# Batch 1's 4x4 normalisation carried out during batch 0's attention, its products and sums on GpSimd

## What is computed

```python
# layer 0
x = x + attention0(xn) + streams(xn)       # one head of width 128; streams: four of 128 channels
def streams(xn):
    z = (rms_norm(xn) @ W_res.T).reshape(B, T, 4, 4) + H_res_base
    H = sinkhorn(z)                        # 50 iterations: rows, then columns, to sum 1 (tau 0.1)
    H = (1 - g) * eye(4) + g * H           # g = sigmoid(gate)
    mixed = einsum('btij,btjc->btic', H, xn_streams)
    return mixed + einsum('btc,btn->btnc', y, H_post)    # y = (streams weighted by H_pre) @ W_branch
# layer 1
x = x + attention1(xn) + ffn1(xn)          # 32 heads, 8 key-value heads of 128, causal; gated low-rank ffn
```

## Time and profile before

| | us |
|---|---|
| median of three runs | 2467.94 |
| lowest, highest | 2463.57, 2469.21 |
| the profiled execution | 2463.85 |
| its span in the trace | 2461.6 |

### The profile page before, as it was taken

The page is one execution under the profiler, slowest core; times in us unless marked ns, Lnnn a source line. Parts: engine busy times, 40 slices in busy tenths (PEclk is TensorE's granted clock), DMA queues, the critical chain, the costliest instruction groups (busy, mean ns, idle before and its releaser), DMA issues. The chain is left out here.

```text
span 2461.6 us, 35450 instructions
## 1 busy us (share of the span) xinstructions
PE 2233.0 (91%) x11154; PEld 1814.2 (74%) x11154; DVE 1554.9 (63%) x3685; ACT 1046.4 (43%) x2182; POOL 1012.0 (41%) x1038
## 2 busy tenths in 40 slices
PE   5767449899999999999999796999999999999998
PEld 4633137688888888888887684788888888888886
DVE  4289875466666666666766455566565756566665
ACT  4322213354545444454545232444454545454543
POOL 2644351264545455363634100435262525343341
PEclk9878779899999999999999998999999999999999
DMA  9500035501010101101010434201101010101010
GB/s 341 189 9 1 0 140 209 207 26 66 9 65 9 65 26 48 56 17 56 26 48 1 166 131 185 86 27 43 47 21 51 26 56 13 60 9 60 18 38 31
DMA packets 74003, 164.83 MB, mean 67 GB/s; under 512 B 4704, under 2 KB 38880, under 8 KB 67296
## 3 DMA queue, kind: packets, MB, share of 16 engines
q1 hardware_dynamic: 73504, 162.69, 18.8%
q10 hardware_dynamic: 432, 1.32, 0.1%
HBM read 113.14 MB, written 72.61 MB: 75 GB/s over the span
## 5 line engine op out<-in xcount | busy, mean ns | idle before, releaser
L1521 DVE TENSOR_TENSOR pT<-psum,pT 128x512 fp32r<-128x512 f32 x576 | 387.0, 689 | 282.4 <-ACT pT L1562 281.6
L1474 POOL TENSOR_TENSOR probs_even<-probs_even,rinv 128x1024 f32<-128x1024 f32 (+2 forms) x192 | 241.0, 1255 | 677.5 <-DVE rinv L1512 677.5
L1562 ACT ACTIVATE pT<-psum 128x512 fp32r<-128x512 f32 x576 | 329.2, 596 | 299.1 <-PE psum L1615 299.0
L1507 DVE CUSTOM_DVE_ANT_0 psum<-psum,causal 128x256 f32<-128x256 f32 (+7 forms) x512 | 386.0, 767 | 38.1 <-PE psum L95 33.3
L1474 POOL TENSOR_TENSOR probs_odd<-probs_odd,rinv 128x896 f32<-128x896 f32 (+2 forms) x192 | 198.6, 1042 | 303.0 <-DVE rinv L1512 302.9
L1556 ACT ACTIVATE probs_even<-psum,nmax 128x1024 f32<-128x1024 f32 (+3 forms) x256 | 204.5, 799 | 250.1 <-DVE nmax L1507 246.2
L93 PE MATMUL psum<-keys,q 128*128 128x512 f32 (+3 forms) x768 | 265.6, 346 | 3.7 <-DVE q L1495 2.8
L95 PE MATMUL psum<-keys,q 128*128 128x512 f32 (+3 forms) x768 | 262.0, 341 | 0.0
L94 PE MATMUL psum<-keys,q 128*128 128x512 f32 (+3 forms) x768 | 261.9, 341 | 0.0
L93 PE MATMUL psum<-pT,vals 128*128 128x512 f32 x576 | 256.3, 445 | 3.9
L1556 ACT ACTIVATE probs_odd<-psum,nmax 128x896 f32<-128x896 f32 (+3 forms) x256 | 176.7, 691 | 148.1 <-DVE nmax L1507 145.9
(11 more groups left out here) (272 smaller groups left out, 4410.5 us busy)
## 6 DMA issues: line engine op xcount, KB each, us to landing
k_parts<-kv_out SPq DMA_DIRECT2D x32, 512.0 KB, 4.9
wq<-wq_copy SPq DMA_DIRECT2D x16, 1024.0 KB, 4.8
wo<-wo_copy SPq DMA_DIRECT2D x16, 1024.0 KB, 4.8
v_parts<-kv_out SPq DMA_DIRECT2D x32, 512.0 KB, 3.9
keys<-k_parts SPq DMA_DIRECT2D x32, 512.0 KB, 4.8
vals<-v_parts SPq DMA_DIRECT2D x64, 256.0 KB, 3.1
acc<-in_x SPq DMA_DIRECT2D x4, 1024.0 KB, 12.3
xn_later<-xn SPq DMA_DIRECT2D x1, 2048.0 KB, 14.5
```

Source lines behind the costliest of these rows:

```text
L1474: pool.tensor_tensor(p, p, rinv[:, u, h:h + 1].to_broadcast([P, (TB - u) * P]), ALU.mult).then_inc(p_ok, 1)
L1507: dve.tensor_tensor_reduce(out=row, in0=row, in1=causal[:, S - n:S], scale=-1.0, scalar=-2 * MASKED, op0=ALU.add, op1=ALU.min, accum_out=n ...
L1521: dve.tensor_tensor(pT[:, n % PT_SLOTS, 1, :], bank[T_BANK + n % 2], f32(pT[:, n % PT_SLOTS, 0, :]), ALU.subtract).then_inc(t_lo, 1)
L1562: act.activation(pT[:, n % PT_SLOTS, 0, :], bank[T_BANK + n % 2], ACT.Copy).then_inc(t_hi, 1)
```

## The change

Batch 1's half of the normalisation leaves the loop of `layer0_mix`. The loop's parts now have four tiles each, the exponentials of batch 1 are put into buffers of their own (z1, k1), and 27 halves lie between units. The heads of a unit are added 14 halves into the next; those of the last unit fall in the mixing behind the loop. That mixing covers six tiles on VectorE and two (BY_POOL) on GpSimd, which waits for the closed T.

In the attention of batch 0, iterations 0 to 4 carry 20, 20, 18, 20 and 20 half-iterations for batch 1's eight tiles. GpSimd takes one after each scaling it does from u = 1 on (u = 2 in iteration 2): product, sum of pairs, sum of the two. VectorE takes the reciprocal of 32 sums behind its next `norm` step. Before iteration 2 ScalarE takes Ln of both factors, VectorE recentres z1 and ScalarE takes Exp; in iteration 5 VectorE closes T for batch 1. The mixing of batch 1's tiles moves to iterations 5 (three tiles), 6 (three) and 7 (two), one product and one sum after a scaling, with u = 1 included; before, it was one tile an iteration, a product and a sum after head 2 from u = 2 on. Their loads move within `loads`. VectorE's and ScalarE's instructions of batch 0's attention are written out instead of looped.

```diff
@@ -27,6 +27,7 @@
 TAU = 0.1
 SINKHORN_ITERS = 50
 SINKHORN_CHUNK = 25
+LATER_CHUNKS, LATER_HALVES = (20, 29), (20, 20, 18, 20, 20)
...
         def part_of(x, k):
-            return x[:, k * (NT // PARTS):(k + 1) * (NT // PARTS)]
+            return x[:, k * (TB // PARTS):(k + 1) * (TB // PARTS)]
...
-        PER_UNIT = 23
+        PER_UNIT = 27
+        BY_POOL = 2
...
+            pool.wait_ge(mix_ok, 1)
+            for t in range(TB - BY_POOL, TB):
+                x = x1[:, t, :].rearrange("p (i c) -> p i c", i=NS)
+                pool.wait_ge(x1_ok, t + 1)
+                for j in range(NS + 1):
+                    n = 2 * ((NS + 1) * (t - (TB - BY_POOL)) + j)
+                    stream = xn[:, t, j * D:(j + 1) * D] if j < NS else y[:, t, :]
+                    weight = T[:, t, :, j] if j < NS else rw[:, t, 1, :]
+                    if j == NS:
+                        pool.wait_ge(y_ok, t // 4 + 1)
+                    if n:
+                        pool.wait_ge(pooled, n)
+                    pool.tensor_tensor(product[:], stream.unsqueeze(1).to_broadcast([P, NS, D]),
+                                       weight.unsqueeze(2).to_broadcast([P, NS, D]), ALU.mult).then_inc(pooled, 1)
+                    pool.wait_ge(pooled, n + 1)
+                    pool.tensor_tensor(x, x, product[:], ALU.add).then_inc(pooled, 1)
...
-            after(dve.tensor_tensor(Z[:], Z[:], over_cols(v), ALU.subtract))
+            after(dve.tensor_tensor(Z[:, 0:TB], Z[:, 0:TB], wide_cols(v[:, 0:TB]), ALU.subtract))
+            after(dve.tensor_tensor(m.z1[:], Z[:, TB:NT], wide_cols(v[:, TB:NT]), ALU.subtract))
...
@@ -516,16 +537,15 @@
                 unit, k = t // UQ, t % UQ
                 between.setdefault(PER_UNIT * unit + 4 * k, []).append((maximum, t))
                 between.setdefault(PER_UNIT * unit + 4 * k + 3, []).append((invert, t))
-                behind = PER_UNIT * (unit + 1) + 16 if unit + 1 < UNITS else 2 * sum(CHUNKS) - UQ
-                between.setdefault(behind + k, []).append((add_heads, t))
+                between.setdefault(PER_UNIT * (unit + 1) + 14 + k, []).append((add_heads, t))
...
-            mixes = 0
-            last_op = {t: (x1_ok, t + 1) for t in range(NT)}
-            for k in range(0, TB, 2):
+            mixes, at = 0, 2 * sum(CHUNKS)
+            ready = {t: (x1_ok, t + 1) for t in range(NT)}
+            for k in range(0, TB - BY_POOL, 2):
                 for j in range(NS + 1):
                     for t in (k, k + 1):
                         if j == NS:
                             dve.wait_ge(y_ok, t // 4 + 1)
-                        dve.wait_ge(*last_op[t])
+                        dve.wait_ge(*ready[t])
...
-                        last_op[t] = mixed, mixes
+                        ready[t] = mixed, mixes
+                        for step, unit_tile in between.pop(at, ()):
+                            step(unit_tile)
+                        at += 1
+            assert not between, (at, between)
...
-            act.activation(K[:], Z[:], ACT.Exp).then_inc(k_ok, 1)
+            act.activation(K[:], Z[:, 0:TB], ACT.Exp).then_inc(k_ok, 1)
+            act.wait_ge(chain, at + 8)
+            act.activation(m.k1[:], m.z1[:], ACT.Exp)
...
-                        if t == 8:
-                            logs()
                 if unit:
                     act.wait_ge(pv_mm, TB * unit)
                     act.activation(oT[:], bank[6][:], ACT.Copy).then_inc(o_ok, 1)
+                if unit == 1:
+                    logs()
...
+            tiles_of = {5: (0, 1, 2), 6: (3, 4, 5), 7: (6, 7)}
+
+            def halves_of(it):
+                return iter(range(sum(LATER_HALVES[:it]), sum(LATER_HALVES[:it + 1])))
+
+            def first_pause(it):
+
+                return 2 if it == turning else 1
+
+            def factors(half):
+
+                return half + 1 + (half >= 2 * LATER_CHUNKS[0])
...
-            def loads(it, g):
+            def loads(it, g, mixed_now=()):
 
                 sp.wait_ge(q_mm, it * QS + QS)
                 load(wq[:, 1], m.wq_s[g]).then_inc(wq_in, 16)
+                for t in mixed_now[:2]:
+                    later_loads(t + 1)
                 sp.wait_ge(pv_mm, it * TILES + (PV0 + first_tile(4)))
                 for k in range(2):
                     load(vals[:, k, 4:8, :], vals_of(g, k, 1)).then_inc(v_in[1], 16)
+                for t in mixed_now[2:]:
+                    later_loads(t + 1)
...
-                loads(it, it + 1)
-                if mixes_later:
-                    later_loads(it + 1)
+                loads(it, it + 1, tiles_of.get(it, ()) if mixes_later else ())
+            if mixes_later:
+                later_loads(TB - 1)
...
@@ -1454,7 +1504,6 @@
                         pool.wait_ge(mixed, n)
                     pool.tensor_tensor(product[:], stream.unsqueeze(1).to_broadcast([P, NS, D]),
                                        weight.unsqueeze(2).to_broadcast([P, NS, D]), ALU.mult).then_inc(mixed, 1)
-                    yield
                     pool.wait_ge(mixed, n + 1)
                     pool.tensor_tensor(x, x, product[:], ALU.add).then_inc(mixed, 1)
                     yield
@@ -1472,15 +1521,36 @@
                         p = probs[u % 2][:, h, 0:(TB - u) * P]
                         pool.wait_ge(p_inv, it * SC + (REP * u + h + 1))
                         pool.tensor_tensor(p, p, rinv[:, u, h:h + 1].to_broadcast([P, (TB - u) * P]), ALU.mult).then_inc(p_ok, 1)
-                        if h == REP - 2 and 2 <= u:
-                            next(beside, None)
+                        if mixes_later and u >= first_pause(it):
                             next(beside, None)
                 for _ in beside:
                     pass
 
+            def scaling(it):
+
+                for half in halves_of(it):
+                    if half == 2 * LATER_CHUNKS[0]:
+                        pool.wait_ge(k_ok, 1)
+                    pool.wait_ge(factor_ok, factors(half))
+                    pool.tensor_tensor(T1, m.k1[:], over_rows(m.row1) if half % 2 else over_cols(m.col1), ALU.mult).then_inc(scaled, 1)
+                    by = T1.rearrange("p t i j -> p t j i") if half % 2 else T1
+                    pool.wait_ge(scaled, half + 1)
+                    pool.tensor_tensor(m.pairs1[:], by[:, :, :, 0:2], by[:, :, :, 2:4], ALU.add).then_inc(paired, 1)
+                    pool.wait_ge(paired, half + 1)
+                    pool.tensor_tensor(m.sm1[:], m.pairs1[:, :, :, 0], m.pairs1[:, :, :, 1], ALU.add).then_inc(summed, 1)
+                    yield
+
...
+            def mixings(it):
+                if it == mixing_from:
+                    pool.wait_ge(share_ok, 1)
+                for t in tiles_of[it]:
+                    yield from mixing(t)
+                    yield
+                    yield
+
             if mixes_later:
                 for it in range(ITERS):
-                    body(it, it == ITERS - 1, mixing(it))
+                    body(it, it == ITERS - 1, scaling(it) if it < mixing_from else mixings(it))
...
-            def body(it, last):
+            def factor(half):
+
+                dve.wait_ge(summed, half + 1)
+                dve.reciprocal((m.col1 if half % 2 else m.row1)[:], m.sm1[:]).then_inc(factor_ok, 1)
+
+            def recentre():
+                dve.wait_ge(logs_ok, 2)
+                dve.tensor_tensor(m.z1[:], m.z1[:], over_rows(m.lrow1), ALU.add).then_inc(z_ok, 1)
+                dve.wait_ge(z_ok, 1)
+                dve.tensor_tensor(m.z1[:], m.z1[:], over_cols(m.lcol1), ALU.add).then_inc(z_ok, 1)
+                dve.memset(m.col1[:], 1.0).then_inc(factor_ok, 1)
+
+            def finish():
+
+                mix = T1.rearrange("p t i j -> p t (i j)")
+                dve.wait_ge(factor_ok, factors(halves))
+                dve.tensor_tensor(T1, m.k1[:], over_rows(m.row1), ALU.mult).then_inc(share, 1)
+                dve.wait_ge(share, 1)
+                dve.tensor_tensor(T1, T1, over_cols(m.col1), ALU.mult).then_inc(share, 1)
+                dve.wait_ge(share, 2)
+                dve.tensor_scalar(mix, mix, m.gate[:, 2:3], None, ALU.mult).then_inc(share, 1)
+                dve.wait_ge(share, 3)
+                dve.tensor_scalar(mix[:, :, 0:NZ:NS + 1], mix[:, :, 0:NZ:NS + 1], m.gate[:, 3:4], None, ALU.add).then_inc(share_ok, 1)
+
+            def body(it, last, beside=iter(())):
...
                         h = arg[1]
                         dve.wait_ge(p_exp, it * SC + (REP * u + h + 1))
                         dve.reciprocal(rinv[:, u, h:h + 1], rsum[:, u, h:h + 1]).then_inc(p_inv, 1)
+                        if mixes_later and (u, h) == (1, 0):
+                            if it == turning:
+                                recentre()
+                            if it == mixing_from:
+                                finish()
                         if h == REP - 1:
 
                             p = probs[u % 2][:, h, 0:(TB - u) * P]
```

(58 more changed lines are left out.)

25 lines of the change are left out of this document (16 added, 9 removed).

## The result

The changed kernel takes 2485.09 us (median of 4 runs, 2483.41 to 2487.2), the kernel before 2468.57 beside it: ratio 1.0069, 95% interval 1.005 to 1.0088. It is slower by 17 us, where 15 had been worked out. Its profiled execution took 2483.41 us, with a span of 2481.6.

The account below looks back on a forecast made before the run. VectorE was taken to bound the first layer's loop and tail, TensorE batch 0's attention. Loop -30, tail +11 and attention +34 made +15: 2479 us on the profiled execution, 2483 on the median, range 2457 to 2502.

Parts of the forecast that it names:

- The bound: VectorE sets the pace in the first layer's loop and tail; in batch 0's attention only TensorE and its waits count.
- The sum, +15: Whole kernel: loop -30, tail +11 and attention +34 give +15 us, 2483 us on the median; chance 0.5.
- The loop, -30: First layer's loop: half-iterations shorten from 1.20 to 0.90 us; -30 us in all, bounds -20 to -35.
- Rival C: First layer's loop: TensorE takes over, only 15 of the 30 us come; +30, 2498 us; chance 0.12.
- The tail, +11: Mixing of batch 0: VectorE's multiply-adds held up beside GpSimd's instructions, 53 us; +11, bounds -8 to +16.
- Rival A: Tail: sharing SBUF costs nothing, the tail ends in 34 us; -4 in all, 2464 us; chance 0.14.
- Iterations 0 to 4, +19: Batch 0's attention: VectorE waits for GpSimd's deferred sums, delaying TensorE; 4.0 us in iterations 0, 1, 3, 4, 2.9 in 2.
- Iterations 5 to 7, +15: Batch 0's attention: mixing steps delay the last wo split, TensorE waits 4.6 us three times, plus 0.7 twice at u = 7.
- The moved DMAs, nothing: Attention: next keys queue behind a load 2 us later than today, but are needed only late; no cost.
- Loops written out, nothing: VectorE's and ScalarE's instructions of batch 0's attention written out: no cost, bounds -1 to +3.
- B: Batch 0's attention swallows the deferred work, TensorE loses at most 5 us; -14 in all, 2454 us; chance 0.14.
- D: GpSimd's small strided sums cost 0.6 us each, a half 1.8; +28 on the forecast, 2511 us; chance 0.1.

Follow-up runs that it names:

- tail_dve: The changed kernel, but VectorE mixes all eight tiles of batch 0 and GpSimd none (BY_POOL = 0); 2481.47 us, ratio 1.0062 to the kernel before.
- mix_u2: The changed kernel, but in iterations 5 to 7 GpSimd's mixing begins at u = 2, behind the wo splits; 2483.34 us, ratio 1.0071 to the kernel before.
- quiet_all: The changed kernel with VectorE mixing all batch 0, batch 1's VectorE loop written out, batch 1's mixing and deferred halves moved; 2441.07 us, ratio 0.9907 to before.

## Why the prediction was right, point by point

- **The bound.** That only TensorE's waits count in the attention, and VectorE in the loop and the tail, held: each wait that an experiment removed there gave its time back, unless another one stood behind it.
- **The sum, +15: measured +17 by the medians, +20.0 by the two spans.** Its closeness is partly luck: the attention took 41.1 us more for 34 (in the iterations of the table), the loop gave 2.7 more than forecast.
- **The loop, -30: measured -32.7.** The reduce takes 0.21 us on average and the reciprocal 0.25, for 0.30 and 0.35 in the earlier trace rows. Rival C, TensorE taking over, fell: 18 of its 105 us moved under the tail, and the other 87 fit into 125. VectorE's waits for it at the additions of heads came to 6.4 us, for 4.4 before.
- **The tail, +11: measured +11.4, for the reason given.** While GpSimd mixes, VectorE gets 24 instructions done beside GpSimd's 20, 25.23 us. I had taken 20 to 40. The plain sum of both engines' work had made it 58; the trace shows 4.5 us less. Of VectorE's 23 multiply-adds there, 20 end 0.15 us behind one of GpSimd's instructions, less than the 0.265 that one takes alone, and GpSimd's are no longer than elsewhere (1.05 and 1.26 us). The Trainium skill (SBUF — State Buffer, Who interferes with whom), from which that estimate came, has one engine blocked until the other's instruction ends; the trace agrees but for this overlap. Rival A fell.
- **Iterations 0 to 4, +19: measured +20.2, by a partly other sum.** At u = 1 the waits were 1.9 us of TensorE (forecast 2.1), the mechanism as described. At u = 7 they were 0.5 instead of 1.2, elsewhere an iteration lost 1.0 instead of 0.7. What filled the gap is a term that I didn't have: the fall of the clock behind the waits at u = 1, 1.5 us in two of the four in this execution (none in that of `tail_dve`, whose code there is the same). The closeness of the sum owes something to luck.
- **Iterations 5 to 7, +15: measured +20.9; this is the term that was mis-sized.** The three waits on the wo splits were 13.8 us, exactly as worked out from the earlier trace rows. What was missing: the clock behind them, 2.4 + 1.6 + 1.5 us, and the closing products of the deferred normalisation on VectorE at u = 1 of iteration 5, for which transposes waited 0.87 and 0.44. For u = 7 I had 1.4; there are three waits of 0.4 for a scaling. These terms make 21.9; other places gave 1 back. I had priced a wait at its own length, which is too little where TensorE's clock falls behind it.
- **The moved DMAs, nothing: right for the change as it is.** But it held by little: `mix_u2`, which mixes later, made the keys wait 5.1 us behind the same load.
- **Loops written out, nothing.** Right: `quiet_all` runs at 113.2 us in iterations 5 and 6 with VectorE's and ScalarE's loops of batch 0 written out. I hadn't thought of the opposite, that a loop left rolled can become slower by what is put ahead of it.
- **Rivals B and D.** B (the attention swallows the work) is wrong for the places chosen, yet nearly right for others: `quiet_all` is its case, and it was to decide at u = 1 and the last split, as B said. Its 0.3 us of TensorE's waits in 113 were one of two such waits: before waits 0.6 us in that window. D fell: the small sums took 0.36 and 0.26 us on average.

## What to carry to other kernels

Work put under an engine that is 99% busy is not free for fitting into another engine's idle total: it has to stand where that engine is idle and where nobody waits for what is queued behind it, and the DMAs that its steps release have to stand behind the ones needed sooner. When a wait is removed, the next one takes its place, so look for all of them before moving anything. And price a TensorE wait with the slower matmuls that may follow it, and a VectorE–GpSimd split of work on SBUF tensors with nearly the sum of both (53.5 of 58 us here).

## What the runs showed of the hardware that I had not expected

- GpSimd's fills of SBUF tiles leave VectorE's multiply-adds at 0.265 us each; beside its products and sums of the same size one gets through per 1.05 us. With one input in PSUM VectorE isn't held either: 0.63 and 1.09 us beside a scaling of 1.68 (above, from 592.70). With two in SBUF even a single instruction in the attention was: the recentring's second addition ended with GpSimd's scaling, 1.69 us for 128 elements.

```profile
707.92 1.69 DVE L1577 TENSOR_TENSOR later_z<-later_z,later_lcol 128x128 f32<-128x128 f32 x1
707.78 1.68 POOL L1523 TENSOR_TENSOR probs_odd<-probs_odd,rinv 128x896 f32<-128x896 f32 x1 [2.02 <-DVE rinv L1606]
```

- After waits of 4.4 to 4.7 us, or of 1.45 and 0.45 close together, TensorE's granted clock fell from 2.4 to 1.2 GHz and stayed low for some 3 to 5 us of matmuls. The same short waits had no such effect in iterations 0 and 3, and in other kernels they had it in other iterations or in none; why, no run settles.
- A rolled loop that nobody edited cost 8.8 us over its seven turns once 40 instructions had been added ahead of it on the same engine, and nothing once written out.
